# The experts' second product in fp32, and the expert rows added by VectorE, in a two-layer transformer kernel on one core

## What is computed

```
logits = x @ Wg + bg                      # x: normalised, Wg: 128 x 8
sel    = the two experts with the largest logits
gates  = softmax(logits where sel, else -inf)
for e in range(8):
    h   = relu(x @ W1[e] + b1[e])         # 128 -> 512
    y   = h @ W2[e] + b2[e]               # 512 -> 128
    out = out + gates[..., e:e+1] * y
x = x + attention(x) + out                # then layer 1
```

## Time and profile before

| what | value |
|---|---|
| median of 3 runs | 1743.77 us (1741.61 to 1750.14) |
| the profiled execution | 1751.61 us |
| its span | 1749.9 us |
| busy: TensorE, VectorE, ScalarE, GpSimd | 88%, 69%, 60%, 47% |
| mean granted clock of TensorE | 0.949 of full |
| chain that ended last | TensorE 61%, VectorE 11%, ScalarE 10%, GpSimd 6%, DMA 3% |
| DMA | 159.35 MB, mean 91 GB/s |

### The profile page before, as it was taken

One profiled execution on the slowest core, in us unless ns is written; L12 is line 12 of the kernel. 1 busy time (PEld: TensorE's weight loads), 2 busy tenths in 40 slices (PEclk: granted clock), 3 DMA queues, 4 the chain that ended last, 5 costly groups with the idle time before them and its releaser, 6 DMA issues.

```text
span 1749.9 us, 33947 instructions
## 1 busy us (share of the span) xinstructions
PE 1539.8 (88%) x11449; PEld 655.0 (37%) x11449; DVE 1202.1 (69%) x3135; ACT 1055.2 (60%) x2322; POOL 817.4 (47%) x728
## 2 busy tenths in 40 slices
PE   2587799889999999999999999999899999889877
PEld 1353353235333543345333543345333533232222
DVE  6553578667885789667975788678976677477523
ACT  2273375667657766676656765677557765736542
POOL 4246355435644555454645455354654461513142
PEclk9998698999999999999999999999999999979877
DMA  5851471136211541236212631145203620201010
GB/s 210 259 152 50 128 195 33 46 93 181 79 42 61 154 118 55 67 93 180 63 34 75 166 103 48 63 117 157 69 29 96 185 80 7 61 13 37 0 37 6
DMA packets 138876, 159.35 MB, mean 91 GB/s; under 512 B 15744, under 2 KB 100304, under 8 KB 137808
## 3 DMA queue, kind: packets, MB, share of 16 engines
q1 hardware_dynamic: 134608, 148.79, 29.1%
q0 software_dynamic: 4096, 8.40, 1.6%
HBM read 115.96 MB, written 40.85 MB: 90 GB/s over the span
## 4 chain that ended last, share of the span: by engine, by line
PE 61%; DVE 11%; ACT 10%; issue 8%; POOL 6%; DMA 3%; SPq 2%; POOLq 0%; ACTq 0%; DVEq 0%
PE banks L450 58%; DVE negmax L862 6%; ACT probs L1202 3%; ACT hm L1271 3%; POOL psums L1423 2%; DMA qkc<-relm 1%; ACT L1202 1%; DVE h L1086 1%; PE banks L714 1%; POOL halves L1379 1%; PE banks L667 1%; SPq L1554 1%; POOL w L1442 1%; ACT h L1320 1%; DVE h L1081 0%
## 5 line engine op out<-in xcount | busy, mean ns | idle before, releaser
L1202 ACT ACTIVATE probs<-banks 128x512 f32<-128x512 f32 (+3 forms) x1216 | 582.5, 534 | 362.1 <-PE banks L450 340.2
L862 DVE TENSOR_REDUCE negmax<-banks 128x1 f16<-128x512 f32 x768 | 491.9, 685 | 157.5 <-PE banks L450 153.9
L858 DVE CUSTOM_DVE_ANT_0 scr<-banks,mask_row 128x384 bf16<-128x384 f32 (+3 forms) x512 | 230.2, 487 | 156.0 <-PE banks L450 146.0
L450 PE MATMUL banks<-kp,qs 32*128 32x512 f16 (+3 forms) x1024 | 239.6, 360 | 64.4 <-DMA kp<-relk 21.1
L450 PE MATMUL banks<-probs,vp 128*32 128x512 f32 (+3 forms) x2048 | 241.1, 544 | 0.2 <-POOL probs L1375 0.2
L450 PE MATMUL banks<-qs,kp 32*128 32x512 f16 (+3 forms) x1024 | 218.3, 352 | 23.3 <-ACT probs L1202 15.9
L1463 POOL TENSOR_TENSOR h_lo<-h,h_hi 128x512 f16<-128x512 f32 x96 | 114.5, 1211 | 211.8 <-ACT h_hi L1314 116.0
L1403 POOL TENSOR_TENSOR hl<-hm,hh 128x512 f16<-128x512 f32 x120 | 139.9, 1168 | 136.3 <-DVE hh L1028 136.3
L1423 POOL TENSOR_TENSOR psums<-psums,probs 128x1024 f32<-128x1024 f32 x64 | 149.2, 2356 | 113.1 <-PE banks L450 113.1
L1271 ACT ACTIVATE hm<-banks,wt 128x128 f32<-128x128 f32 x480 | 137.7, 374 | 72.2 <-PE banks L450 71.7
L450 PE MATMUL banks<-qkc 97*128 97x512 f16 (+1 forms) x512 | 169.6, 404 | 8.8 <-DVE negmax L862 3.0
(11 more groups left out here) (211 smaller groups left out, 2457.1 us busy)
## 6 DMA issues: line engine op xcount, KB each, us to landing
wt<-wexp SPq DMA_DIRECT2D x120, 258.0 KB, 3.0
wt<-wexp SPq DMA_DIRECT2D x120, 256.0 KB, 3.0
qkc<-relm SPq DMA_DIRECT2D x96, 128.0 KB, 3.2
qs<-relq SPq DMA_DIRECT2D x64, 128.0 KB, 2.5
kp<-relk SPq DMA_DIRECT2D x64, 128.0 KB, 2.6
relm<-halves SPq DMA_DIRECT2D x32, 256.0 KB, 2.1
xg<-xslots SPq DMA_DIRECT2D x24, 256.0 KB, 3.0
yslots<-yv SPq DMA_DIRECT2D x24, 256.0 KB, 3.5
```

The costliest lines, as they stand in the source:

```text
L450: return nc.tensor.matmul(psum[rows_, bank, cols_], lhsT, rhs, start=start, stop=stop)
L858: v.tensor_tensor_reduce(scr[:, s, 0:kw], psum[:, SCO + s, 0:kw], mask_row[:, T - kw:T], -1.0, 3e38, ALU.add, ALU.min, negmax[:, g.n % 2, ...
L862: v.tensor_reduce(negmax[:, g.n % 2, NC * h + c:NC * h + c + 1], psum[:, SCO + s, 0:kw], AX.X, ALU.max, negate=True).then_inc(sem("max"), 1)
L1202: a.activation(keys(g, c)[:, 2 * pair + s, q0:T], psum[:, TRA + s, q0:T], ACT.Exp, scale=SCALE[main(g)]).then_inc(sem("exp"), 1)
```

## The change

`down` takes `hm` and W2 in fp32, four matmuls in place of twelve. `hm` gets a third buffer; VectorE's cast, GpSimd's subtraction, `hh`, `hl` and `wexp2` go. W2 is read from the input `split_in` itself (rows of 2 KB, as in `wexp2`), so its two chunks are neither loaded, split nor stored at the start. ScalarE's scaling and TensorE's identity products go; in a new piece `add` at step 55 VectorE multiplies the gathered rows by `gk` and adds them to x, before `wo0_out` adds the attention's output. The gathers of the next batch wait for that piece.

Many steps are shifted. The largest: `scatter` from -16, -15, -16, -15 to -27, -26, -25, -24; `pick` from -10 to -24; the first two `xg_load` from -5, -4 to -22, -21; `slots` from -25 to -27; the first loads of W1 by two steps later; the remaining chunks' `split` from 7, 21, 35 to 9, 21, 35.

```diff
-AT.update({("scatter", i): at for i, at in enumerate((-16, -15, -16, -15), 0)})
+AT.update({("scatter", i): at for i, at in enumerate((-27, -26, -25, -24), 0)})
-AT.update({("xg_load", i): at for i, at in enumerate((-5, -4, 7, 19), 0)})
+AT.update({("xg_load", i): at for i, at in enumerate((-22, -21, 7, 19), 0)})
-AT.update({("w_store", i): at for i, at in enumerate((-11, -10, -4, 2), 0)})
+AT.update({("w_store", i): at for i, at in enumerate((-11, -10), 0)})
-AT.update({("scale", i): at for i, at in enumerate((52, 51), 0)})
-AT.update({("split", i): at for i, at in enumerate((-12, -11, -2, 3, 7, 21, 35), 0)})
+AT.update({("split", i): at for i, at in enumerate((-12, -11, 9, 21, 35), 0)})
...
                 def down(b, t):
                     n = NT * b + t
-                    pe.wait_ge(sem("h_lo"), n + 1)
+                    taken(pe, "u", ("up", t), b)
...
-                    w = wt2[:, n % 3, :].bitcast(F16)
-                    last = three(N, ch(t % 4), [(hh[:, n % 2, ch(hc)], hl[:, n % 2, ch(hc)],
-                                                 w[:, P * hc:P * hc + P], w[:, 512 + P * hc:512 + P * hc + P])
-                                                for hc in range(HC)])
+                    for hc in range(HC):
+                        last = mm(N, ch(t % 4), hm[:, n % 3, ch(hc)], wt2[:, n % 3, P * hc:P * hc + P], hc == 0, hc == HC - 1)
...
                         for c in range(NC):
-                            mm(M, ch(c), oT[:, ch(c)], W("l0_o"), False, False)
-                        pe.wait_ge(sem("scaled"), 2 * b + 2)
-                        for k in range(2):
-                            last = mm(M, slice(0, T), C("ident"), yg[:, NC * k:NC * k + NC, :].rearrange("p c d -> p (c d)"), False, k == 1)
+                            last = mm(M, ch(c), oT[:, ch(c)], W("l0_o"), False, c == NC - 1)
...
-                    for t in range(NT):
-                        if (b := due(G - 1, ("up", t))) is not None:
-                            n = NT * b + t
-                            taken(dve, "u", ("up", t), b)
-                            if n >= 2:
-                                dve.wait_ge(sem("down"), n - 1)
-                            v.tensor_copy(hh[:, n % 2, :], hm[:, n % 2, :]).then_inc(sem("hh"), 1)
+                    if (b := due(G, "add")) is not None:
+                        dve.wait_ge(sem("gath"), 128 * (b + 1))
+                        for k in range(2):
+                            for c in range(NC):
+                                ins = v.scalar_tensor_tensor(out=xs[:, b % 4, c, :], in0=yg[:, NC * k + c, :],
+                                                             scalar=gk[:, k, c:c + 1], in1=xs[:, b % 4, c, :],
+                                                             op0=ALU.mult, op1=ALU.add)
+                            if k == 0:
+                                link(ins)
+                        ins.then_inc(sem("x_moe"), 1)
+                        dve.wait_ge(sem("x_moe"), b + 1)
...
-                            if n >= 2:
-                                act.wait_ge(sem("h_lo"), n - 1)
+                            if n >= 3:
+                                act.wait_ge(sem("down"), n - 2)
...
-                                ins = a.activation(yg[:, NC * k + c, :], yg[:, NC * k + c, :], ACT.Copy, scale=gk[:, k, c:c + 1])
...
-                            p_.tensor_tensor(out=hl[:, n % 2, :], in0=hm[:, n % 2, :], in1=hh[:, n % 2, :],
-                                             op=ALU.subtract).then_inc(sem("h_lo"), 1)
...
-                                    full(pool, "m", "wo0", b - 1)
+                                    pool.wait_ge(sem("x_moe"), b)
...
+                w2_rows = split_in[:, W2_AT:W2_AT + E * 512].rearrange("p (e f) -> e p f", f=512)
...
-                    sp.dma_start(wt2[:, n % 3, :], wexp2[bass.ds(e, 1), :, :].rearrange("e p f -> (e p) f")).then_inc(sem(f"wdn{n % 3}"), 16)
+                    sp.dma_start(wt2[:, n % 3, :], w2_rows[bass.ds(e, 1), :, :].rearrange("e p f -> (e p) f")).then_inc(sem(f"wdn{n % 3}"), 16)
```

More of the change, by code:

```diff
@@ L81 @@
 A1_AT = (120, 128, 136, 152)
-MOVE = {"route": {0: 6}, "warm0": {-1: -6}, "warm1": {-1: 6}, "front": {}, "prep": {0: 11},
-        "ca": {-1: -24}, "mid": {-1: -24}, "last": {-1: -30}, "ffn": {-1: -24}, "tail": {-2: -12, -1: -52}}
+MOVE = {"route": {0: 6}, "warm0": {}, "warm1": {}, "front": {}, "prep": {0: 11}, "ca": {-1: -24},
+        "mid": {-1: -24}, "last": {-1: -30}, "ffn": {-1: -24}, "tail": {-2: -12, -1: -52}}
 @dataclass
@@ L135 @@
 AT.update({("h1_out", i): at for i, at in enumerate((152, 157, 167, 180), 0)})
[L136 to L138 removed]
+AT.update({("up", i): at for i, at in enumerate((10, 12, 13, 16, 17, 20, 22, 24, 25, 29, 30, 32, 34, 36, 38), 0)})
@@ L139 @@
+AT.update({("down", i): at for i, at in enumerate((13, 15, 17, 19, 21, 23, 25, 27, 29, 31, 33, 35, 37, 39, 42), 0)})
+AT.update({("wup", i): at for i, at in enumerate((7, 9, 7, 11, 12, 15, 17, 19, 21, 25, 25, 25, 29, 31, 33), 0)})
 AT.update({("wdn", i): at for i, at in enumerate((9, 11, 13, 15, 17, 19, 21, 23, 25, 27, 29, 31, 33, 35, 37), 0)})
-AT.update({("scatter", i): at for i, at in enumerate((-16, -15, -16, -15), 0)})
+AT.update({("scatter", i): at for i, at in enumerate((-27, -26, -25, -24), 0)})
@@ L154 @@
+AT.update({("load", i): at for i, at in enumerate((-2, 11, 21), 2)})
 AT.update({("fa", i): at for i, at in enumerate((133, 135, 137, 139), 0)})
@@ L371, in build @@
         h32 = sb("h32", [P, HC, T])
[L372 to L374 removed]
+        hm = sb("hm", [P, 3, T])
+        cmps = sb("cmps", [P, 2, T], F16)
         sel = sb("sel", [P, NC, E], F16)
@@ L391, in build @@
         gates = sb("gates", [P, NC, E])
-        cmp1, cmp2 = (hh[:, k, :].bitcast(F32).rearrange("p (c e f) -> p c e f", e=E, f=E) for k in range(2))
+        cmp1, cmp2 = (cmps[:, k, :].bitcast(F32).rearrange("p (c e f) -> p c e f", e=E, f=E) for k in range(2))
         am, cons = r_a[0:16, 128:256], r_a[0:16, 256:257]
@@ L418, in build @@
         CH = GH * T
-        LOADS = [(at, min(CH, n_split - at)) for at in range(0, n_split, CH)]
+        W2_AT, _ = SPLIT_AT["W2"]
+        LOADS = [(at, min(CH, n_split - at)) for at in range(0, n_split, CH) if not W2_AT <= at < FIRST_F]
         NW = len(LOADS)
-        other = h_hi[:, :, :, :].rearrange("p a h t -> p (a h t)").bitcast(F32)
-        HOME = [stage[:, 0, :], stage[:, 1, :], late, other, late, late, late]
-        EARLY = 4
+        HOME = [stage[:, 0, :], stage[:, 1, :], late, late, late]
+        EARLY = 2
         def staged(n):
             return HOME[n][:, 0:LOADS[n][1]]
-        flat = psums[:, :, :].rearrange("p h t -> p (h t)").bitcast(F16)
-        spare = h_lo[:, :, :, :].rearrange("p a h t -> p a (h t)")
         HALF = [*(w[:, :, :].rearrange("p k f -> p (k f)")[:, 0:CH // 2].bitcast(F16) for w in (wt1, wt2)),
-                hm[:, :, :].rearrange("p k t -> p (k t)").bitcast(F16), yg[:, :, :].rearrange("p a d -> p (a d)").bitcast(F16),
-                flat[:, 0:CH], flat[:, CH:2 * CH], spare[:, 0, :], spare[:, 1, :]]
-        STORED_W = 16 * 9
+                hm[:, 0:2, :].rearrange("p k t -> p (k t)").bitcast(F16), yg[:, :, :].rearrange("p a d -> p (a d)").bitcast(F16)]
+        STORED_W = 16 * 5
         def half(n, k):
@@ L962, in pick @@
                     link(ins)
-                    if b:
-                        dve.wait_ge(sem("scaled"), 2 * b)
-                    v.tensor_reduce(gk[:, :, :], first[:, :, :, :], AX.X, ALU.add).then_inc(sem("gk"), 1)
-                    dve.wait_ge(sem("gk"), b + 1)
+                    link(v.tensor_reduce(gk[:, :, :], first[:, :, :, :], AX.X, ALU.add))
                 def gate_weights(b):
@@ L1398, in experts @@
                                                       xr[:, c, :, :].rearrange("p a d -> p (a d)"), None).then_inc(sem("scat"), 16)
-                    for t in range(NT):
-                        if (b := due(G - 1, ("up", t))) is not None:
-                            n = NT * b + t
-                            pool.wait_ge(sem("hh"), n + 1)
-                            p_.tensor_tensor(out=hl[:, n % 2, :], in0=hm[:, n % 2, :], in1=hh[:, n % 2, :],
-                                             op=ALU.subtract).then_inc(sem("h_lo"), 1)
                     for c in range(NC):
```

44 lines of the change are left out of this document (17 added, 27 removed), and 4 rows, old and new, of the table AT.

## The result

The changed kernel takes 1762.2 us (median of 4 runs, 1760.4 to 1766.8) where the kernel before, on the same chip, takes 1744.1 (4 runs). The ratio is 1.0102 [1.0081, 1.0122]: 1.0% slower, or 17.8 us, against a forecast of 1764 and +20. The two profiled executions differ by less, 1761.2 to 1751.6 us, because that of the kernel before lies 7.5 us above its median and that of the changed one does not.

A forecast was written before the change was run, and what follows sets the result against it. TensorE was taken to bound the steady batches, waiting only 13.7 us per batch. Terms +27 + 7 - 10 + 0 - 4 = +20 us gave 1764 us, range 1738 to 1788.

The forecast's parts named there:

- A: Second product `down` as four fp32 matmuls instead of twelve fp16: 0.26 us more each, +27 us over seven steady batches.
- C: Eight additions of expert rows on VectorE at step 55: 2.2 us alone, 4.3 us with waiting for GpSimd.
- D: Casts leave VectorE, subtractions GpSimd, scalings ScalarE: 1.5 us per batch comes back, -10 us (0 to -26).
- E: Shifted steps, chiefly scatters on GpSimd: zero, with 1 us to spare, up to +2 us per batch if margin missed.
- F: First batch: scatters +3, fewer splits -2, stretch around `wo0` -4, `down` -1; sum -4 us (-9 to +6).
- the prediction's own sign of being wrong: Forecast wrong if fp32 `down`s fit into waits, or VectorE or GpSimd stops TensorE around step 55 to 62.
- B: Identity products of `wo0` leave TensorE: 1.8 us per batch saved; together with the additions on VectorE, +7 us.
- the lock: VectorE's additions at step 55 held up by GpSimd's simultaneous operations; the first addition waits some 2.1 us.
- The prediction's worst case: Additions at step 55, if only VectorE counts: `slots`, `addresses` and the next silu start 3.6 us later.
- the six signs to look for: `down` 0.9-1.1 us; TensorE busy +2, period +3; additions following GpSimd; `wo0` without waits; first scores near 55; fewer maxima waits.
- Rival 1: VectorE paces every batch, its relief shows in waits before scores: a gain, 1727 us; chance 0.13.
- Rival 2: Additions alternate with GpSimd's at step 55, scatters start later: 2 to 3 us more per batch, 1779 to 1786; chance 0.17.

The follow-up runs named there:

- fp16_down: Changed kernel with `down` again as twelve fp16 matmuls reading constants, without cast and subtraction, output not computed: 1739.5 us, 0.9986 of the kernel before.
- no_additions: Changed kernel with the eight additions cut to one operation of 8 columns, expert rows not added: 1737.4 us, 0.9968 of the kernel before.
- only_fp32_down: Kernel before with `down` in fp32, no casts or subtractions, old steps, scalings and identity products kept: 1762.3 us, ratio 1.0108.
- late_scatters: Changed kernel with scatters, `xg_load` and `pick` back at their old steps, `slots` still at -27: 1756.9 us, 1.0063 of the kernel before.
- only_additions: Kernel before with the eight additions at step 55 replacing scalings and identity products, other steps old: 1763.6 us, ratio 1.0119.
- additions_after_slots: As only_additions on the kernel before, but with `slots` moved from -25 to -27, ahead of the additions: 1768.0 us, ratio 1.0125.

## Why the prediction was right, and where it wasn't

The time (1764 for 1762.2) and the sign are right, and the term that decides both, A, by the mechanism that was named. That the sum comes within 2 us is partly luck: C and D were both larger than said, E wasn't zero, and two parts of F missed and cancelled. And the prediction's own sign of being wrong appeared beside it: VectorE does stop TensorE around step 55 to 62, for 0.78 and 1.09 us in six of the seven steady batches.

One view serves several terms: the six periods from the router of the second batch to that of the eighth, in the kernel before, the changed one, fp16_down, no_additions and only_fp32_down (length, then TensorE's busy time; the number before the DMA's share is the granted clock):

```profile
147.73:1226.27 1078.54, 988.57 (x7833) 436.00 (x7831) 793.80 (x2186) 695.54 (x1590) 551.78 (x508) 0.97 0.34 97
143.13:1235.62 1092.49, 991.17 (x7447) 457.59 (x7445) 772.30 (x2143) 682.99 (x1542) 444.14 (x418) 0.96 0.33 96
142.22:1219.78 1077.56, 972.40 (x7807) 434.74 (x7805) 775.12 (x2143) 681.69 (x1542) 443.70 (x418) 0.96 0.33 97
143.09:1213.48 1070.39, 977.73 (x7447) 452.35 (x7445) 760.23 (x2100) 681.62 (x1542) 443.59 (x418) 0.98 0.34 98
146.82:1235.74 1088.92, 1003.80 (x7473) 457.82 (x7471) 757.48 (x2097) 695.10 (x1590) 447.42 (x418) 0.97 0.33 96
```

The terms one by one:

- **A, +27 us.** The mechanism is right, and so is the step: 0.26 us per `down` by the means (1.03 for 0.77 in fp16_down), 0.23 by the medians, where I took 0.26 from the earlier trace rows. The time shows less, 20 us (15.5 to 24.5), just under my lower edge of 22. The rest seems to fall into waits: in the view above TensorE stands still for 101 us in the changed kernel and for 105 in fp16_down. The Trainium skill's four passes for fp32 (FP8 and Floating Point Precision, TensorE Precision Notes) gave an estimate of 0.23 us, and the trace agrees with it (0.23 to 0.26).
- **B and C, +7 us.** The sum came out near, +11, but the step under it failed: I put the additions ahead of `slots`, while `slots` had moved to step 53 and stands ahead of them. In six of the seven steady batches of the changed kernel they take 2.6 us, nearly clear of the lock, once 4.44 (at 1453.43, beside `psums`). What they cost is 3.3 us per batch, by two things that I didn't have. In the view above the changed kernel is 22 us longer than no_additions, with the same 7447 matmul records: 9 us of it are waits, and for 13 TensorE is busy longer with the same work, at a granted clock of 0.96 for 0.98. (That trace is the fastest of the twelve runs of no_additions, 1729.5 us, so it gives the kinds of the cost and not their sizes.) The prediction's worst case was also added up wrong: 2.1 + 2.2 us make 4.3 for `slots`, as it says itself behind it, and not 3.6; the middle would be 1.25 us per batch, 9 us in place of 7. B is the one part of it taken over from the prediction unmeasured.
- **D, -10 us.** 14 us, give or take 7.5. Right in size. Whether it is a constant of the work removed is open: only_fp32_down sheds the same casts and subtractions and still costs 18.8 us, 1 us under A's 20, but both have intervals of over 4 us, and in the view above TensorE stands still there for 85 us where it did for 90. So some relief is there too; that it is worth more where VectorE and GpSimd have been loaded with additions and early scatters is a guess that these runs allow and don't show.
- **E, 0.** Low by some 4 us, if by anything: the shifted scatters cost 7 (give or take 5.6), of which 3 belong to the first batch and stood under F. The margin of 1 us that I had worked out was for scatters from 678 to 688.4; `idx` came behind the additions, and they ran from 683.1 to 693.0. The upper bound of +2 us per batch holds.
- **F, -4 us.** Right in size, by parts that missed and cancelled. The second batch's router reaches VectorE at 143.13 in the timeline of the changed kernel, for 147.73 before: 4.6 us earlier, at a place ahead of `wo0`, up to which my terms had +3 - 2 - 1 = 0. Within it the scatters made the first scores 2.9 us later (55.09 for 52.16; 51.85 in late_scatters), I had said 3. The -4 us around `wo0` came nearly whole, its bank reaches xs at 163.01 for 170.99, and was lost again: VectorE's next normalisation waits 8.09 us for `rstd`, which GpSimd makes at 175.99, behind the second batch's eight scatters (162.86 to 172.83) and a key sum. Before, that wait was 1.17 us, and `xn` comes only 3.6 us earlier, at 177.06 for 180.68.

```profile
143.13 0.19 DVE L969 TENSOR_TENSOR lg<-banks,rows 128x32 f32<-128x32 f32 x1 [12.58 <-PE banks L444]
163.01 0.69 DVE L1034 TENSOR_TENSOR xs<-xs,banks 128x512 f32<-128x512 f32 x1
177.06 1.11 DVE L872 TENSOR_SCALAR xn<-xs,mv,rstd 128x128 f32<-128x128 f32 x4 [8.09 <-POOL rstd L1406]
```

With F the measured terms make 20 + 11 - 14 + 4 - 4 = 17 us, for 17.8. That agreement proves little: their intervals add up to some 11 us (the root of the sum of squares), B is in it unmeasured, and each price is that of one part taken out of the changed kernel, while the halves of the change don't add.

From the router of the second batch to that of the eighth the changed kernel loses 13.9 us in six batches, 2.3 each, where the terms gave 3.4.

Of the six signs to look for, four came: `down` at 1.0 us, the period 3.5 us longer (with 3.2 of TensorE's busy time, where I had 2), `wo0` without waits, and the first scores at 55. One came in part: only the first addition is held by a GpSimd operation, and for 0.3 us, where I had 2.1. One did not: the waits for maxima are the same 54 us. Rival 1 had the waits for maxima as what VectorE's relief would shorten; they didn't move, which is why it fell. Rival 2 described, in the main, what only_additions does, not what the changed kernel does.

## What to carry to other kernels

When a change moves work onto an engine that is two thirds busy, its price is set by what stands behind it in that engine's order: here the same eight instructions cost 21, 8 or 4 us by their step. Take the order from the changed schedule, not from the old one, and follow every wait that you remove to the next reader; it was `late_f`, then `g_t`, then `xs`. And price a relief together with the load that comes in its place, since the two need not add: the halves of this change cost 19 and 21 us apart and 18 together. The nearest pair at the same steps for scatters and `slots` says the same: only_fp32_down and additions_after_slots cost 19 and 22 us, and late_scatters, which has both, 11 (the other small shifts of steps are in it).

## What the runs showed of the hardware

A short wait can cost more than its length through TensorE's clock. The table of stages of the changed kernel around the waits of 0.78 and 1.09 us, and then the same matmuls of `wide,oT` in the kernel before:

```profile
684.00:687.00 3.00, 1.86 (x8) 0.51 (x6) 2.90 (x10) 1.09 (x3) 2.09 (x4) 1.00 0.13 44
687.00:691.00 4.00, 3.99 (x20) 2.48 (x23) 3.17 (x5) 1.81 (x4) 3.08 (x4) 0.57 0.15 49
```

```profile
679.00:683.00 4.00, 4.00 (x21) 1.97 (x19) 2.71 (x5) 1.95 (x4) 1.16 (x1) 1.00 0.00 0
```

TensorE had been busy for 1.86 of 3 us, and the granted clock of the next 4 us is 0.57, most of it at the lower level of 1.2 GHz, where it was 1.00 before. At 0.57 the 4 us lose some 1.7. `wide,oT` takes 1.05 us in all seven steady batches of the kernel before, in no_additions and in only_additions, but 1.78 to 1.92 in five of seven in the changed kernel (and in fp16_down, so A isn't the reason), in three of seven in late_scatters, and in all seven of additions_after_slots. So part of what the additions at step 55 cost, up to 5 x 1.7 = 8 us at this place in the changed kernel, is paid in clock and not in waits, and the view of the waits doesn't list it. The same two waits are no sure sign of it: they stand ahead of the `wide,oT` at 307.3 and at 884.6 too, which take 1.05 us.

That one group of matmuls doesn't tell the whole, though. With the additions at 58 `wide,oT` takes 1.05 us too, and the clock falls behind it instead, after the wait of 3.58 us for `xs` that ends at 689.3:

```profile
690.00:697.00 7.00, 6.67 (x29) 2.48 (x27) 5.13 (x9) 3.29 (x6) 2.39 (x2) 0.51 0.14 39
```

Nor does the clock tell the changed kernel from the one before: over their whole profiled executions it is 0.951 and 0.949. The profiled execution of no_additions has 0.965, but its twelve runs lie between 0.940 and 0.965. All this was read from the traces; no run changed the clock by itself.
